# An mLSTM stage on one core: values by v as weights in two column groups, and the result turned back

## What is computed

```python
def _mlstm_head(q, k, v, ig, fg, eps=1e-06):
    s, dh = q.shape
    log_f = jax.nn.log_sigmoid(fg)
    cs = jnp.concatenate([jnp.zeros((1, 1), log_f.dtype), jnp.cumsum(log_f, axis=0)], axis=0)
    neg = jnp.asarray(-0.7 * jnp.finfo(cs.dtype).max, cs.dtype)
    log_d = jnp.where(jnp.tri(s, dtype=bool), (cs - cs.T)[1:, 1:] + ig.T, neg)
    m = jnp.max(log_d, axis=-1, keepdims=True)
    d = jnp.exp(log_d - m)
    c = q @ (k.T / jnp.sqrt(dh)) * d
    n = jnp.maximum(jnp.sum(c, axis=-1, keepdims=True), jnp.exp(-m))
    return c / (n + eps) @ v
...
var = jnp.mean(jnp.square(h.astype(jnp.float32)), axis=-1, keepdims=True)
h = (h * jax.lax.rsqrt(var + 1e-06)).astype(h.dtype) * (1.0 + rms_scale)
```

## Time and profile before

| | us |
|---|---|
| median of 3 runs | 698.41 |
| lowest, highest | 696.13, 700.05 |
| the profiled execution | 698.65 |
| its span, first to last instruction | 696.9 |
| mean granted clock of TensorE over the span | 0.778 |
| the stage, first decays to last division | 88.9 to 153.1 |
| TensorE busy, VectorE, ScalarE, GpSimd, over the span | 514.7, 340.1, 211.0, 222.4 |

### The profile page before, as it was taken

The page is one execution under the profiler, slowest core; times in us unless marked ns, Lnnn a source line. Parts: engine busy times, 40 slices in busy tenths (PEclk is TensorE's granted clock), DMA queues, the critical chain, the costliest instruction groups (busy, mean ns, idle before and its releaser), DMA issues.

```text
span 696.9 us, 12794 instructions
## 1 busy us (share of the span) xinstructions
PE 514.7 (74%) x4709; PEld 404.9 (58%) x4709; DVE 340.1 (49%) x1045; ACT 211.0 (30%) x431; POOL 222.4 (32%) x333
## 2 busy tenths in 40 slices
PE   3367789997769995864879999899784875574910
PEld 1135568886359981623856666666563774574910
DVE  4646535677633314066234556566842454342632
ACT  3020553322115650432523444344231331121300
POOL 4501035652731008111103333233166006244044
PEclk9577955555659996797967999999775888795965
DMA  9970100000168111001300111111021401331132
GB/s 241 346 220 1 36 26 2 1 0 1 49 114 56 37 44 45 17 1 45 140 1 1 18 17 16 17 17 9 9 42 51 102 16 53 107 88 36 47 84 63
DMA packets 114716, 38.60 MB, mean 55 GB/s; under 512 B 76768, under 2 KB 112224, under 8 KB 114016
## 3 DMA queue, kind: packets, MB, share of 16 engines
q1 hardware_dynamic: 111440, 31.30, 19.1%
q0 software_dynamic: 3072, 6.30, 3.1%
q10 hardware_dynamic: 144, 0.19, 0.1%
HBM read 22.45 MB, written 15.34 MB: 54 GB/s over the span
## 4 chain that ended last, share of the span: by engine, by line
PE 51%; DVE 22%; issue 12%; POOL 4%; ACT 4%; DMA 3%; another core or an unknown queue 2%; DVEq 1%; SPq 0%; POOLq 0%; ACTq 0%
PE bank L1221 6%; PE bank L1384 5%; PE bank L1097 4%; PE bank L1366 4%; DVE first_max_of L1876 4%; PE bank L1400 3%; PE bank L1168 3%; PE bank L1179 3%; PE bank L1264 2%; PE bank L1098 2%; PE bank L1279 2%; DVE XN L1434 2%; POOL rstd L641 2%; DVE first_max_of L1875 2%
## 5 line engine op out<-in xcount | busy, mean ns | idle before, releaser
L754 POOL TENSOR_SCALAR_AFFINE_SELECT score_room<-score_room 128x256 f32<-128x256 f32 x128 | 48.2, 408 | 127.1 <-ACT score_room L918 127.1
L918 ACT ACTIVATE score_room<-bank 128x1152 f32<-128x1152 f32 (+1 forms) x43 | 48.3, 1124 | 100.9 <-PE bank L1282 97.4
L641 POOL TENSOR_TENSOR rstd<-vareps,power 128x4 f32<-128x4 f32 x24 | 24.5, 1019 | 123.4 <-DVE vareps L1426 123.2
L1384 PE MATMUL bank<-sel_room 128*128 128x128 f32 x368 | 56.2, 302 | 0.5 <-issue 0.2
L1400 PE MATMUL bank<-ctxT,h_room 128*128 x184 | 33.7, 312 | 29.2 <-issue 19.7
L1875 DVE TENSOR_REDUCE first_max_of<-bank 128x3 f32<-128x384 f32 (+1 forms) x43 | 23.9, 555 | 60.1 <-PE bank L1369 60.1
L1384 PEld LDWEIGHTS bank<-sel_room 128*128 128x128 f32 x368 | 51.2, 215 | 2.4 <-issue 0.9
L776 POOL DMA_INDIRECT w_room<-part_outputs,f_rows x32 | 30.8, 962 | 59.0 <-DMA part_outputs<-sel_room 49.8
L1400 PEld LDWEIGHTS bank<-ctxT,h_room 128*128 128x128 f32 x184 | 28.0, 218 | 31.3 <-issue 31.2
L1888 DVE TENSOR_TENSOR h_room<-bank,h_room 128x256 f32<-128x256 f32 x46 | 19.5, 424 | 50.1 <-issue 27.5
L1279 PE MATMUL bank<-QM,w_room 32*128 32x256 f32 x256 | 38.0, 434 | 6.1 <-DVE QM L1865 5.2
(11 more groups left out here) (276 smaller groups left out, 1151.7 us busy)
## 6 DMA issues: line engine op xcount, KB each, us to landing
w_room<-in_w SPq DMA_DIRECT2D x2, 2048.0 KB, 11.2
part_rows<-OV SPq DMA_DIRECT2D x2, 1472.0 KB, 16.7
part_outputs<-sel_room SPq DMA_DIRECT2D x10, 256.0 KB, 2.3
scan_room<-in_w SPq DMA_DIRECT2D x1, 2048.0 KB, 7.8
slot_rows<-OV SPq DMA_DIRECT2D x1, 1472.0 KB, 17.0
score_room<-slot_rows SPq DMA_DIRECT2D x5, 256.0 KB, 5.2
slot_outputs<-XNT SPq DMA_DIRECT2D x5, 256.0 KB, 2.3
w_room<-part_rows SPq DMA_DIRECT2D x5, 256.0 KB, 4.2
```

The lines of the kernel that those rows point to most:

```text
L641: pool.tensor_tensor(rstd[:, t0:t1], vareps[:, t0:t1], power[:, 0:1].to_broadcast([P, CT]), ALU.pow).then_inc(rstd_ready, 1)
L754: last = pool.affine_select(cells, cells, [[0, 2], [1, P]], ALU.is_ge, 0.0, base=0, channel_multiplier=-1)
L918: act.activation(pT[:, v % RING, 0:n, :], banks(3, n)[:, :, 0:CUT], ACT.Exp, scale=float(AD) ** -0.5).then_inc(e_p, 1)
L1384: last = pe.matmul(ps[n % 2][:, k * P:(k + 1) * P], w12_now[:, n % 2, k * P:(k + 1) * P], turned, start=True, stop=True)
```

## The change

Values are made the other way round. v is the weights (128 keys by 64 columns: 32 of v, the ones, and 31 columns of whatever lies next in `v_room`), c is moving (256 columns for i = 0, 128 for i = 1). Heads 2q and 2q + 1 write partitions 0 to 63 and 64 to 127 of bank 6, which are two column groups of the array. The result has head and feature on the partitions, so ScalarE copies the bank to SBUF (`OB`, new `copy_values`) and PE turns it with four transposes into bank 7 (new `b_turn_values`), which the division reads. Bank 6 is written again only after the copy, `OB` only after the turn, bank 7 only after the division. The decays move out of `b_scores` into `b_decays`, and those of batch b + 1 stand between values(b - 1) and the turn of batch b - 1. One memset of 64 columns of `v_room` is added at the start of POOL's queue.

```diff
+        OB = h_room[:, 4 * CUT:4 * CUT + 2 * S]
...
+            pool.memset(v_room[:, T * NH * (HD + 1):T * NH * (HD + 1) + HW], 0.0)
...
+            def copy_values(b):
+
+                act.wait_ge(b_pv, b + 1)
+                if b >= 1:
+                    act.wait_ge(b_ot, b)
+                act.activation(OB, ps[6][:], ACT.Copy).then_inc(b_ov, 1)
...
+                if u % 2 == 1 and u >= 2:
+                    copy_values(u // 2 - 1)
+            copy_values(B - 1)
...
-                if b == 1:
+                else:
+                    pe.wait_ge(b_ov, b)
+                for q in range(2):
+                    for i in range(2):
+                        for f in range(2):
+                            h = 2 * q + f
+                            at = ((2 * b + i) * NH + h) * (HD + 1)
+                            last = pe.matmul(ps[6][HW * f:HW * (f + 1), q * S + i * P:(q + 1) * S], v_room[:, at:at + HW],
+                                             cT[:, (NH * b + h) % (2 * NH), i * S:CUT if i else S], start=(i == 0), stop=(i == 1))
+                last.then_inc(b_pv, 1)
+
+            def b_turn_values(b):
+
+                pe.wait_ge(b_ov, b + 1)
+                if b == 0:
                     pe.wait_ge(c_bsumc, 1)
-                if b >= 2:
-                    pe.wait_ge(b_div, b - 1)
-                for h in range(NH):
-                    weights = cT[:, (NH * b + h) % (2 * NH), :]
+                else:
+                    pe.wait_ge(b_div, b)
+                for q in range(2):
                     for i in range(2):
-                        n = NH * i + h
-                        o = ps[6 + b % 2][:, n * HW:n * HW + HD + 1]
-                        pe.matmul(o, weights[:, i * P:(i + 1) * P], vaug[:, 2 * b, h, :], start=True, stop=(i == 0))
-                    last = pe.matmul(o, weights[:, S:CUT], vaug[:, 2 * b + 1, h, :], start=False, stop=True)
-                last.then_inc(b_pv, 1)
-
+                        n, m = 2 * i + q, 2 * q + i
+                        last = pe.transpose(ps[7][:, n * P:(n + 1) * P], OB[:, m * P:(m + 1) * P], ident)
+                last.then_inc(b_ot, 1)
+
+            b_decays(0)
             for b in range(B):
                 b_scores(b)
                 if b >= 1:
                     b_values(b - 1)
+                if b + 1 < B:
+                    b_decays(b + 1)
+                if b >= 1:
+                    b_turn_values(b - 1)
             b_values(B - 1)
+            b_turn_values(B - 1)
...
-                o = ps[6 + b % 2][:].rearrange("p (n d) -> p n d", d=HW)
-                dve.wait_ge(b_pv, b + 1)
+                o = ps[7][:].rearrange("p (n d) -> p n d", d=HW)
+                dve.wait_ge(b_ot, b + 1)
```

More of the change, by code:

```diff
@@ L326, in build @@
         b_pv = sem("b_pv")
+        b_ov = sem("b_ov")
+        b_ot = sem("b_ot")
         b_div = sem("b_div")
@@ L1055, in _, with b_decays @@
             last.then_inc(b_turn, 1)
-            def b_scores(b):
-                i0 = b * S
+            def b_decays(b):
                 if b == 0:
@@ L1070, in b_scores @@
                     last.then_inc(b_dk, 1)
+            def b_scores(b):
+                i0 = b * S
                 if b >= 1:
```

## The result

The changed kernel took 690.53 us (median of 4 runs, 689.59 to 693.63) beside 698.7 us (4 runs, 696.13 to 700.05) for the kernel before: a ratio of 0.9895, 95% interval 0.9853 to 0.9937. The forecast was 687.3 us in a range of 682.0 to 692.5, so the time lies inside the range and the gain is 8.2 us where 11.2 were expected. By the time alone the rival of half clock throughout, priced at 690.4, would look right; the trace is what rules it out.

The account below looks back on a forecast made before the run. PE at half clock was taken to bound the mLSTM stage. Full clock's -13.9 - 2.4 + 0.9 = -15.4 us, less 2.5, 1.2 and 0.5 for slow batches, gave -11.2: 687.3 us from the median, range 682 to 692.5.

Parts of the forecast that it names:

- half clock throughout: Rival: PE's granted clock stays at 0.50 all through the mLSTM stage; -8.0 us in sum, 690.4 us; chance 0.18.
- What bounded the kernel: mLSTM stage: the chain of waits never leaves PE, 7.71 us a batch at granted clock 0.50; stage to become 50 to 54.
- The values: PE's values matmuls, per batch: 5.12 us becomes 2.72 at half clock (-2.40), 1.44 at full clock.
- The turn and the copy: Four PE transposes: +0.85 us a batch at half clock, +0.43 at full; ScalarE's copy 0.61, exposed twice at 0.8 each.
- The decays "cost 0": PE's decays matmuls in the mLSTM stage: the same matmuls one slot earlier, costing 0.
- the mixed case: mLSTM stage's clock begins at 0.50, rises in two or three batches, falls back at times; -11.2 us, 687.3; chance 0.56.
- The periods: mLSTM batches, scores to scores: 6.16 us at half clock; at full clock 4.5 plain, 6.9 with statistics, 6.0 in batches 5, 7.
- The stage's end and the tail: Last scores to end of mLSTM stage: -1.5 us at half clock, -2.4 at full; norm tail behind it gives back +0.9.
- Everything later hangs on the routing, so it shifts as a whole: All work after the mLSTM stage's norm and routing: moves earlier by the full gain, with no loss later.
- the gain is lost later: Rival: after the shorter stage, a later stretch loses some 8 us by its clock, or a transfer keeps its time; 695-699; chance 0.08.
- full clock throughout: Rival: mLSTM stage at full clock from the first batches on; -15.4 us in sum, 683.0 us; chance 0.11.
- Groups in a row: Rival: the values' two column groups run one after the other on PE, 8.72 us a batch; +10.6 us, 709; chance 0.07.

Follow-up runs that it names:

- e2: The changed kernel with the column-group loop outermost, so all four matmuls of one group stand ahead of the other's; ratio 0.9882 to the kernel before.
- e5: The kernel before with only the decays moved: those of batch b + 1 directly behind the scores of batch b, ahead of the values; ratio 1.0075.
- e7: The kernel before with 128 moving columns per values matmul and the next batch's decays directly behind the scores, ahead of the values; ratio 0.9902.
- e4: The kernel before with 128 moving columns in each values matmul instead of 33, results over banks 6 and 7, no copy or turn; ratio 0.9893.
- e3: The kernel before with 64 moving columns in each values matmul instead of 33, in the one bank, no copy or turn; ratio 1.0022.
- e0: The changed kernel run again unedited, for a second trace; ratio 0.9876 to the kernel before.
- e1: The changed kernel with the decays of batch b back ahead of its scores, the turn directly behind the values; ratio 0.9889 to the kernel before.

## Why the prediction was right, and where its sum was not

- **What bounded the kernel**: right. PE ruled the stage at half clock; with PE's work and its clock changed the stage fell from 64.2 to 51.0 us, inside the 50 to 54 forecast.
- **The values**: right. 2.72 was forecast at half and 1.44 at full clock, 2.83 and 1.52 came in the timeline. e2 shows that 2.83 needs the alternating order.
- **The turn and the copy**: right. 0.85 and 0.43 plus a drain were forecast, 1.06 to 1.12 and 0.66 with the drain came; the copy is 0.60 and exposed by 0.70 at batches 6 and 7 (0.8 forecast).
- **The decays "cost 0"**: right for the place where they stand, but not for the reason's breadth. e5 and e7 show a cost of 2.3 to 2.5 us one step further ahead.
- **The clock**: the mixed case came, as forecast: 0.50 in the first batches, 1.00 from 100 us on, falls behind the norm's batches. The reason, that c streams through the array where before weights were loaded for 33 columns, held in its direction: e4 streams 128 columns and its clock rose. In e3, with 64, it did not, so what decides is not settled.
- **The periods**: from scores to scores the changed kernel has 6.18, 4.60, 4.35, 6.96, 5.64 and 6.72 us. The first is the half-clock period forecast at 6.16, the plain ones were put at 4.5, those with the statistics at 6.9, the one between at 6.0. Together they are 34.5 against 46.2 before: -11.8, where the mixed case had -9.7 (its -13.9 with 2.5, 1.2 and 0.5 given back). The term that was mis-sized is what the slow batches cost: forecast 4.2, in fact 34.5 - 32.4 = 2.1, since the clock had risen by the third batch.
- **The stage's end and the tail**: from the last scores to the last division 12.9 became 11.4, -1.6 (forecast -1.5 at half clock, where it ran; the mixed sum had taken the -2.4 of full clock, 0.8 too much). From the last division to the routing 14.9 became 15.8, +0.9 (forecast +0.9). With 0.2 more between the first decays and the second scores that is -11.8 - 1.6 + 0.9 + 0.2 = -12.3, where the forecast's sum was -11.2.
- **"Everything later hangs on the routing, so it shifts as a whole"**: this is the step whose size failed in the profiled pair. Routing came 12.2 us sooner against its own first decays, and 13.6 against the start of the execution, since its first decays began 1.4 us sooner. The projections of layer 1's scan still began 13.4 us sooner, but they took 25.8 us instead of 23.2. Some 0.9 of that came back in between, and the last mixture gave back another 2.7: the last matmuls of L1400 and L1435 are 9.0 us apart. The rows are these, projections first (before, after), then the mixture:

```profile
L1205 PE MATMUL bank<-XNT,lw x24: 592/592/1061, 294.5 to 317.7; 128*128 128x512 f32 x24
...
L1400 PE MATMUL bank<-ctxT,h_room x184: 275/275/577, 545.6 to 665.2; 128*128 x184
```

```profile
L1240 PE MATMUL bank<-XNT,lw x24: 592/686/1220, 281.1 to 306.9; 128*128 128x512 f32 x24
...
L1435 PE MATMUL bank<-ctxT,h_room x184: 275/275/578, 533.9 to 656.2; 128*128 x184
```

  The granted clock in 300 to 304 us, which in the changed kernel is the end of these projections, was 0.53; the kernel before had 1.00 at their end (314 to 318 us). This looks like the rival "the gain is lost later" in small, but the runs don't tie it to the change: e0, the same kernel, had 23.4 us for those projections, and e1 and e2, with the new values too, 23.2 each. From the last of layer 1's values to the last of the mixture e0 had 132.7 us where the changed kernel had 137.7, the kernel before 135.0, and e3, nearly the kernel before, 134.3. So these stretches vary by some 3 us with the execution, in either kernel. The 8.2 us measured is a gain of some 12 at the routing less such a draw. That it was this draw in the timed runs too was only argued: one execution of each was traced.
- **The rivals**: half clock throughout and full clock throughout did not come (0.75 in the mean), although the first one's 690.4 us is next to the measured 690.53: that is chance, a larger gain in the stage less the draw above. "Groups in a row" was made in part in e2 and cost 1.2 to 1.6 us in the stage, not a loss of 10: its price was worked out with no overlap at all, where half of the records still ran in pairs, and at half clock, where the clock rose. The price of a rival belongs to the state that the rival itself brings about.

## What to carry to other kernels

A matmul stage that is busy all the time at half clock is bound by its clock as much as by its work, and a change can be worth having for raising it, apart from the cycles it saves; e4 got the stage's whole gain by streaming columns that nobody reads. Once PE is no longer the bound, look at the order on the engines around it: the power that POOL took longest over was worth 1.3 us, and the place of the statistics 3.2. When the same work is moved ahead in a queue, the wait that it carries moves too, and decides.

## What was not expected of the hardware

- Moving operands of 64 columns left the granted clock at 0.50 with PE busy throughout (e3), and with 128 columns it rose to 1.00 (e4), at the same number of matmuls and with a record as long as before at half clock (0.213 us).
- Two column groups with their matmuls in a row still took only 4.16 us at half clock, under the 5.28 of no overlap that the prediction worked out: the second group's first four records ran beside the first group's last four, ahead of their turn in the queue (e2).
- The part ahead of the stage is the same code in all kernels, yet the first decays began between 85.5 and 92.9 us. The kernel before took 694.67 us on one chip and 650.58 and 650.92 on two others, and the traces on the latter put most of it in two stretches outside the mLSTM: from layer 1's key projections to its scan 16 to 18 us instead of 37 to 39, and the last mixture 110 to 113 instead of 133 to 138. Why was not tried.
